# Visiting the 32-column matmuls of an attention kernel once for two key steps

## The reference

```python
q = (hidden_states @ Wq).reshape(b, s, NUM_HEADS, HEAD_DIM)
kv = hidden_states @ Wkv
k, v = (kv[..., :HEAD_DIM], kv[..., HEAD_DIM:])
scores = jnp.einsum('bqhd,bkd->bhqk', q, k) * scale
...
scores = jnp.where(causal[None, None], scores + bias[None], -jnp.inf)
attn = jax.nn.softmax(scores, axis=-1)
out = jnp.einsum('bhqk,bkd->bqhd', attn, v).reshape(b, s, h)
return out @ Wo
```

## Time and profile before

| what | value |
|---|---|
| median of three executions | 4188.78 us |
| profiled execution | 4190.77 us, span 4189.0 us |
| PE busy | 3813.9 us, 91% of the span |
| DVE, ACT, POOL busy | 59%, 46%, 32% |
| mean PEclk | 0.953 |
| the two batches' attention | to about 3283 us |
| feed-forward part | the rest, some 906 us |
| L794 (PV and row sums) | 5120 and 3200 matmuls, 617.2 and 363.3 us busy |

### The profile page before, as it was taken

One profiled execution on the slowest core, in us unless ns is written; L12 is line 12 of the kernel. 1 busy time (PEld: TensorE's weight loads), 2 busy tenths in 40 slices (PEclk: granted clock), 3 DMA queues, 4 the chain that ended last, 5 costly groups with the idle time before them and its releaser, 6 DMA issues. The chain is left out here.

```text
span 4189.0 us, 73921 instructions
## 1 busy us (share of the span) xinstructions
PE 3813.9 (91%) x22065; PEld 2365.4 (56%) x22065; DVE 2476.4 (59%) x4462; ACT 1927.4 (46%) x3253; POOL 1359.9 (32%) x420
## 2 busy tenths in 40 slices
PE   5989989999999997798999999999999599999998
PEld 3555554445444443555555444544444288888887
DVE  4556666666766672455776667766665244444444
ACT  2436555565666565344664656566566400000000
POOL 1114434444444454111443444445454200000010
PEclk8889999999999998878999999999999899999999
DMA  2111110000000001111111000000000311111111
GB/s 72 39 49 33 30 41 24 20 22 22 14 19 14 19 6 34 54 42 44 32 28 41 22 22 22 14 19 14 19 14 6 131 56 60 60 60 60 60 60 51
DMA packets 159069, 152.11 MB, mean 36 GB/s; under 512 B 8388, under 2 KB 141508, under 8 KB 156584
## 3 DMA queue, kind: packets, MB, share of 16 engines
q1 hardware_dynamic: 158696, 147.70, 11.9%
HBM read 96.75 MB, written 33.62 MB: 31 GB/s over the span
## 5 line engine op out<-in xcount | busy, mean ns | idle before, releaser
L509 ACT ACTIVATE prob<-ps_s,alibi 128x512 f32<-128x512 f32 (+3 forms) x2560 | 1522.6, 623 | 1206.5 <-PE ps_s L771 613.3
L589 DVE TENSOR_REDUCE mxp<-ps_a 128x1 f32<-128x512 f32 (+3 forms) x2560 | 1460.1, 605 | 864.2 <-PE ps_a L710 445.2
L452 POOL TENSOR_TENSOR prob<-prob 128x2048 f32<-128x2048 f32 (+1 forms) x240 | 1043.7, 4349 | 1209.4 <-ACT prob L509 1209.3
L771 PE MATMUL ps_s<-qst,kexp 97*128 97x512 f32 (+3 forms) x2560 | 1103.1, 442 | 133.8 <-ACT prob L509 96.1
L707 PE MATMUL ps_a<-kmax,qst 97*128 97x512 f32 (+3 forms) x2560 | 962.1, 402 | 32.6 <-DVE mxp L589 14.9
L771 PEld LDWEIGHTS ps_s<-qst,kexp 97*128 97x128 f32 x2560 | 498.0, 196 | 814.8 <-ACT prob L509 531.6
L794 PE MATMUL ps_o<-prob,val 128*32 128x512 f32 (+3 forms) x5120 | 617.2, 555 | 7.5 <-ACT prob L509 7.5
L707 PEld LDWEIGHTS ps_a<-kmax,qst 97*128 97x128 f32 x2560 | 505.3, 199 | 111.2 <-DVE mxp L589 56.6
L794 PE MATMUL ps_sum<-prob,ones 128*32 128x512 f32 (+3 forms) x3200 | 363.3, 527 | 0.0
L980 POOL TENSOR_TENSOR hb_sb<-h_sb,bias_b 128x1024 f32<-128x1024 f32 x32 | 76.8, 2401 | 791.4 <-DVE z_sb L1124 732.3
L607 DVE RECIPROCAL r_sb<-s_sb 128x128 f32<-128x128 f32 x256 | 233.8, 931 | 123.8 <-ACT s_sb L515 121.6
(11 more groups left out here) (148 smaller groups left out, 3710.6 us busy)
## 6 DMA issues: line engine op xcount, KB each, us to landing
wq_raw<-in_L_attn_Wq SPq DMA_DIRECT2D x65, 512.0 KB, 3.7
xs<-in_L_attn_hidden_states SPq DMA_DIRECT2D x9, 2048.0 KB, 8.2
qst<-qst SPq DMA_DIRECT2D x64, 256.0 KB
att_scratch<-at_sb SPq DMA_DIRECT2D x64, 256.0 KB, 2.3
at_raw<-att_scratch SPq DMA_DIRECT2D x32, 512.0 KB, 5.4
x_sb<-in_L_attn_hidden_states SPq DMA_DIRECT2D x32, 512.0 KB, 4.3
out<-z_sb SPq DMA_DIRECT2D x32, 512.0 KB, 3.2
z_sb<-in_L_attn_Wo SPq DMA_DIRECT2D x4, 512.0 KB, 5.6
```

What stands on the lines that cost most here:

```text
L452: nc.gpsimd.tensor_tensor(even[:, :, c1:], even[:, :, c1:], odd[:, :, c1:], ALU.add).then_inc(pair_done, 1)
L509: nc.scalar.activation(prob[slot][:, h, c0:], ps_s[bank][:, c0:], ACT.Exp, bias=alibi_of(u, h, k - QT * s)).then_inc(e_done, 1)
L589: nc.vector.tensor_reduce(mxp[:, h * QT + t, c:c + 1], ps_a[bank][:, 0:cols], AX.X, ALU.max).then_inc(a_done, 1)
L771: last = nc.tensor.matmul(ps_s[bank][:, c0:], kexp[0:KR, k * P:(k + 1) * P], qst[buf][0:KR, h, c0:], start=True, stop=not diagonal)
```

## The change

Only the list of `plan_step` changes. The visits in odd key steps go. In every even step k from 2 on, after the second score, the list now has `PV` of steps k-2 and k-1 together, then the row sums due. At the end of a unit it has both last `PV`, then the last pair's `SP`, then the two last `SM`. No instruction is added or taken away; the waits of each stay what they were.

```diff
-            if k and h == 1:
-                out.append(("PV", k - 1))
+            if k and k % 2 == 0 and h == 1:
+                out += [("PV", k - 2), ("PV", k - 1)]
                 if k > 2 * summed:
-                    out.append(("SM", k - 1))
-                if k >= 4 and k % 2 == 0 and k // 2 - 2 < summed:
+                    out += [("SM", k - 2), ("SM", k - 1)]
+                if k >= 4 and k // 2 - 2 < summed:
                     out.append(("SP", k // 2 - 2))
...
+    out += [("PV", n - 2), ("PV", n - 1)]
     if summed:
         out.append(("SP", summed - 1))
-    out += [("PV", n - 1), ("SM", n - 1)]
+    out += [("SM", n - 2), ("SM", n - 1)]
```

## The result

| | median us (4 executions) | range |
|---|---|---|
| before | 4186.69 | 4184.06 to 4193.92 |
| after | 4351.68 | 4340.44 to 4362.66 |

(The fourth execution of the kernel before moves its median from 4188.78 to 4186.69 us.) The ratio is 1.0391, 95% interval 1.0355 to 1.0427: the change costs 165 us. The forecast was slower by 26 us, with a range up to 4285 us. The sign was right; the size was six times too small, and the time lies 67 us above the range.

A forecast was written before the change was run, and what follows sets the result against it. The score-exponential loop bounds attention outside the projections. Ordinary units of segments 1 to 3 +43 us, segment 0 -17, last two units and clock 0: +26 on the profiled 4190.8, about 4215 after the median's 2 us; range 4180 to 4285.

The forecast's parts named there:

- What bounds the kernel: Attention outside the projections: the loop of score, exponential, score sets the pace, 1.54 us for any further two tiles.
- Projection steps: Visit of step 1, where PE is the limit, goes: -0.30 us in each unit of segments 1 to 3.
- Plain and diagonal pairs: Two key steps each: plain, 8.39 to 8.49 us (+0.10); diagonal, narrower tiles with mask matmuls, taken 0.
- the next pair: Pair after the one with query copies, holding one more copy and a DVE reciprocal: +0.40 us, between +0.10 and +0.69.
- The shift: Unit end: DVE's shift comes 0.08 us ahead of POOL's sum, so PE's 0.87 us wait vanishes.
- The end of a unit: Last six narrow tiles, uninterrupted by visits, replace the shift wait: 5.34 to 5.77 us, +0.43.
- ends at half clock: Rival: a quarter of 48 unit ends in segments 1 to 3 fall, 5.2 us each, +62 us, 4277; chance 0.10.
- The copy pairs: Two key steps in which ACT copies the next unit's queries: 8.54 to 9.23 us, +0.69.
- the term for the clock: Granted clock at unit ends and in segment 0: ends -83 us and +62 us, taken 0.
- the last two units of a segment: 12 units mixing the other terms with input projections: taken 0, bounds -10 and +15 us.
- Segment 0: Two of four visits go (-0.60), a 0.47 us wait is covered: -1.07 us in each of 16 units, -17 us.
- segment 0 loses its half clock: Rival: over half of segment 0's 16 units stay at full clock, -42 to -83 us, 4132 to 4173; chance 0.12.

The follow-up runs named there:

- Numbers 6 and 7: 6: number 5 with the old unit end in segments 1 to 3, 4142.23 us; 7: kernel before, step n-3's visit dropped and new end there, 4238.98 us.
- Number 2: The changed kernel with each score matmul for the maxima in slots 9 to 25 issued twice (820 added): 4330.82 us, ratio 1.0346.
- number 5: The changed kernel with query copies, weight split and first reciprocals moved into slots ending in a visit, segments 1 to 3 except unit 6: 4210.48 us.
- number 1: The kernel before with the change in segment 0 alone; segments 1 to 3 as before: 4157.65 us, ratio 0.9936.

## Why the prediction was right in sign and wrong in size

**What bounds the kernel: right.** The loop of score, exponential, score bounds the stretches without projections, and merging visits lengthens it: PE's wait for exponentials grew by 73 us. That is why the change doesn't gain what 320 visits at 0.30 us would give.

**Projection steps: right, small.** They take some 12.86 us instead of 13.1 where nothing else happens (-0.25; forecast -0.30); in sum -5.9 instead of -10.8 us.

**Plain and diagonal pairs: right.** 8.47 to 8.56 us against 8.49 forecast in the two pairs after the next pair of segment 3; the diagonal moved by 2 us in all. (The sum counts no plain pair in segment 2, but its third pair is one but for its last two tiles; it went from 8.93 to 8.7 us.)

**The shift: right.** It starts 0.20 us ahead of POOL's sum (0.08 by the forecast), takes 0.17 to 0.18 us, and in the ordinary units PE's wait for it is gone. The Trainium skill's page "SBUF — State Buffer", section "Who interferes with whom", says that the one issued first wins. The traces agree in both orders: 0.18 us ahead of POOL's sum, and 2.17 us behind it for the same instruction.

**The end of a unit: its length right, its clock wrong.** 5.6 us at full clock against 5.77 forecast. But 13 of 36 fall to half clock, which costs about 1.35 us each. The rival *ends at half clock* had a quarter of them fall, which is near; its price of 5.2 us, taken from a whole unit of segment 0, was four times too high. Numbers 6 and 7 show what the new end costs once other losses are out of the way: 68 and 74 us, with more ends that fall.

**The copy pairs: mechanism right, the clock missing.** At full clock they take 9.33 to 9.40 us in segment 3 against 9.23 forecast, and the pairs behind them grow by 0.7 where they are clean in segment 2. About 0.8 us for each of 60 pairs is 48 us (an estimate from the 14 copy pairs and the one next pair without a fall) against the 34 forecast: +0.40 for the next pair was too little. The prediction counted a copy and a reciprocal in it and left out ACT's weight split (L474), 1.05 us long against 0.59 for a copy, which stands in the same pair. The remaining 90 us are the clock: 229 us at half speed where before there was none, 0.39 us lost for each.

**The failed step is the term for the clock.** I took it as 0 and looked for falls at the ends of units and in segment 0 only. Measured, it is some 90 us in the copy pairs and the next pairs alone, and over the whole attention part 282 us more at half clock, which at 0.39 us for each would be 110 of the 171 us (an estimate). My own working had put waits of about half a microsecond at each copy, into a stretch in which nothing else of PE's covers the loop, and directly behind it the longest visit of the unit. I did not ask what the clock would do there. Number 2 shows it from one side (more work in the stretch, full clock, shorter pairs), number 5 from the other (the same work in a better place, full clock, pairs of 8.3 to 8.9 us in segments 2 and 3). The ends *given* as -83 us and +62 us for that term did not cover the place either, so the range was too narrow at the top.

**Taken as 0, and not 0: the last two units of a segment.** They cost 40.6 us, outside the bounds of -10 and +15. Half of that is the last unit of segment 3 (+22), where without the maxima PE has least to do: pairs that took 7.4 to 7.5 us before now take 9.2 to 10.3 us.

**Segment 0: right in sign, too small.** -27 instead of -17 us; number 1 confirms the gain. But the forecast had counted the visits and one wait, and what the trace shows is 70 us less at half clock. At 0.39 us for each that alone would be 27 us (an estimate), the whole gain. So no run shows the -1.07 us for each unit, and that the sign came out right may be luck. The rival that segment 0 loses its half clock came true in part: 107 us are left.

**What stays open.** The same code falls in one batch and not in the other (10.12 and 12.64 us above); nothing in the traces that I looked at tells which of two alike pairs will fall. And the last unit of segment 3 keeps slow pairs in numbers 5 and 6; that was not followed further. What in the new end lets the clock fall, its waits or its few matmuls, is open too: no run kept PE busy there, as number 2 did in the copy pairs.

## What to carry to other kernels

Small matmuls spread through a loop do more than their own work: each visit is cover for a wait of the loop around it and keeps PE from standing idle. Before merging them, list what else stands in the uncovered stretch (copies, reciprocals), price each at full clock, then list every place where the kernel runs at half clock already and what PE does ahead of it, and ask whether the change makes new places like these, with the longest block of matmuls right behind them. Merge where PE is the limit and no wait needs the cover (here 55 us), and move small work of other engines to where PE is busy anyway (another 33 us).

## What the hardware showed

- In the copy pair shown, the fall of the clock was dearer than any wait ahead of it: three waits of 0.27, 0.50 and 0.59 us, then a visit of 4.44 instead of 2.70 us. With 820 useless matmuls added to such stretches (number 2), PEclk was 1.00 in all 60 pairs and the loss 148 us instead of 165.
- The clock does not only fall where PE stands still for long. In the copy pair above PE is never idle for more than 0.59 us ahead of the fall.
- DVE's shift of 16 columns took 2.17 us when it started behind POOL's sum and 0.18 us when it started 0.20 us ahead of it. In segment 1 of numbers 5 and 6, with a small copy on DVE moved just ahead of it, it started behind the sum again and took 2.68 to 2.86 us.
